# Routing the last chunk of tokens through the experts' blocks, and single chunks through the shared expert, in a GRU and mixture-of-experts kernel

## The reference, cut to what matters

```python
# x: (8, 256, 512), cond_2048: (8, 512); a GRU over 256 steps, then a mixture of experts on its 2048 states
def cell(h, x):
    gi = x @ W_ih + b_ih
    gh = h @ W_hh + b_hh
    r = sigmoid(i_r + h_r); z = sigmoid(i_z + h_z); n = tanh(i_n + r * h_n)
    return (1.0 - z) * n + z * h
...
topk_w, topk_ids = top_k(softmax(x @ w_gate), 2)          # 8 experts, 2 for each token
topk_w = topk_w / sum(topk_w)
gu = einsum('th,ehf->etf', x, w_gate_up)                  # 512 -> 2 * 256 for each expert
eo = einsum('eti,eih->eth', silu(g) * u, w_down)
routed = einsum('te,eth->th', combine, eo)
shared = silu_and_mul(x @ w_sh_gate_up) @ w_sh_down       # 512 -> 2 * 1024 -> 512
...
y = x + routed + shared
```

## Time and profile before

| | us |
|---|---|
| median of three runs | 1266.33 |
| the runs | 1262.6 to 1267.35 |
| the profiled execution, its device time | 1269.48 |
| its span, first to last instruction | 1267.6 |
| TensorE busy in the span | 1074.9 (85%) |
| VectorE busy | 854.7 (67%) |
| ScalarE busy | 569.2 (45%) |
| GpSimd busy | 226.6 (18%) |
| mean granted TensorE clock | 0.981 |
| share of the 16 DMA engines, GpSimd's queue and SyncE's | 31.9% and 13.4% |

### The profile page before, as it was taken

How to read it: one execution, slowest core, us unless ns; L and a number is a source line. 1 busy time by engine, 2 the same in 40 slices (tenths; PEclk the granted TensorE clock), 3 DMA queues, 4 the chain that set the end, 5 groups by cost and what they waited for, 6 DMA issues and landing times.

```text
span 1267.6 us, 35210 instructions
## 1 busy us (share of the span) xinstructions
PE 1074.9 (85%) x13360; PEld 650.7 (51%) x13360; DVE 854.7 (67%) x3767; ACT 569.2 (45%) x1849; POOL 226.6 (18%) x237
## 2 busy tenths in 40 slices
PE   3789887677988889899899888998899798788997
PEld 2556554455554555455455544554455454444775
DVE  5888887688788787677777775777577667411222
ACT  5755445555454444344444433443344244433332
POOL 0100000201010212211321130113013212342331
PEclk9999999999999999999999998999899999989999
DMA  8923554628164741722371343134314503788652
GB/s 302 411 68 110 209 196 151 138 102 301 38 239 157 192 124 24 261 72 51 39 261 27 60 134 144 19 62 168 107 18 77 217 20 87 270 245 248 185 130 43
DMA packets 66442, 180.74 MB, mean 143 GB/s; under 512 B 7579, under 2 KB 40129, under 8 KB 58817
## 3 DMA queue, kind: packets, MB, share of 16 engines
q0 software_dynamic: 24960, 119.25, 31.9%
q1 hardware_dynamic: 41312, 59.24, 13.4%
HBM read 135.18 MB, written 52.08 MB: 148 GB/s over the span
## 4 chain that ended last, share of the span: by engine, by line
PE 44%; DVE 27%; DMA 11%; issue 9%; ACT 6%; POOL 2%; another core or an unknown queue 0%; DVEq 0%; POOLq 0%; SPq 0%; ACTq 0%
PE psG L693 13%; PE psG L699 11%; DMA arena<-hidden_rows,arena 6%; PE psU L756 5%; DVE arena L1047 4%; DVE arena L1045 4%; DVE arena L1051 3%; PE psU L766 3%; ACT arena L1455 3%; DVE arena L1054 2%; PE psS L825 2%; DVE arena L1056 2%; DVE arena L1064 2%; DVE arena L1068 2%; PE psD L778 2%
## 5 line engine op out<-in xcount | busy, mean ns | idle before, releaser
L693 PE MATMUL psG<-arena 128*32 128x384 f16 x4096 | 216.5, 332 | 95.7 <-DVE arena L1068 89.1
L1451 ACT ACTIVATE arena<-arena 128x32 f32<-128x32 f32 x256 | 58.5, 228 | 343.5 <-DVE arena L1049 339.4
L699 PE MATMUL psG<-arena 128*32 128x384 f16 x4096 | 211.8, 327 | 0.0
L756 PE MATMUL psU<-arena 128*128 128x256 f16 x1536 | 203.1, 279 | 0.2 <-DVE arena L941 0.2
L1045 DVE STREAM_TRANSPOSE arena<-psG 128x128 f32<-128x128 f32 x256 | 80.9, 316 | 176.7 <-PE psG L699 167.8
L693 PEld LDWEIGHTS psG<-arena 128*32 128x32 f16 x4096 | 86.7, 97 | 200.1 <-DVE arena L1068 163.8
L756 PEld LDWEIGHTS psU<-arena 128*128 128x128 f16 x1536 | 148.7, 100 | 51.1 <-issue 12.5
L1661 POOL DMA_INDIRECT y<-arena x53 | 84.6, 1597 | 373.0 <-ACT arena L1565 235.8
L699 PEld LDWEIGHTS psG<-arena 128*32 128x32 f16 x4096 | 110.3, 98 | 57.9 <-issue 1.6
L1047 DVE STREAM_TRANSPOSE arena<-psG 128x256 f32<-128x256 f32 x256 | 104.0, 406 | 0.0
L778 PE MATMUL psD<-arena 128*128 128x512 f16 x384 | 96.4, 382 | 0.0
(11 more groups left out here) (178 smaller groups left out, 1631.3 us busy)
## 6 DMA issues: line engine op xcount, KB each, us to landing
arena<-wgu POOLq DMA_DIRECT2D x32, 512.0 KB, 6.8
expert_weights<-arena POOLq DMA_DIRECT2D x9, 1536.0 KB, 5.7
arena<-expert_weights SPq DMA_DIRECT2D x8, 1536.0 KB, 8.3
gi_scratch<-arena SPq DMA_DIRECT2D x84, 128.0 KB, 2.0
arena<-gi_scratch SPq DMA_DIRECT2D x14, 768.0 KB, 6.6
arena<-wd POOLq DMA_DIRECT2D x16, 512.0 KB, 5.3
arena<-x SPq DMA_DIRECT2D x8, 512.0 KB, 3.8
hidden_rows<-arena SPq DMA_DIRECT2D x15, 256.0 KB, 3.1
```

Source lines behind the costliest of these rows:

```text
L693: e.matmul(psG[32 * j:32 * j + 32, 0:384], prev[:, c, 2:6].rearrange("p q n -> p (q n)"), whv[c][1][:, :, :, 32 * j:32 * j + 32], start=(c ...
L699: r = e.matmul(psG[32 * j:32 * j + 32, 0:384], prev[:, c, 0:4].rearrange("p q n -> p (q n)"), whv[c][0][:, :, :, 32 * j:32 * j + 32], star ...
L756: r = e.matmul(psU[u % 2][:, 256 * gu:256 * gu + N], half(W_GS + ex * 4 + c, pw)[:, o:o + 128], hh[:, 1 - ph, c, 0:N], start=(c == 0 and j ...
```

## The change

- `BOUND` becomes 6, 8, 10, 12, 13, 14, 15, 16, 16. All 16 chunks are routed and filed, chunks 12 to 15 as groups of one. The first seven bounds give the blocks that are sure to be full, 23 (`KS`). Then eight blocks (`STATIC`, to `KD` = 31), one for each expert in fixed order, its next one, full or not; their weights come through `x_weights`. Then eight gathered blocks for what is left (`LAST`, to `NB` = 39), with weights by index.
- All 39 blocks run as blocks did; `HX`, `hx`, `comb`, `x_acc`, `acc_init`, `x_rows` and `y_store` go.
- The shared expert takes chunks 12, 13, 14 and 15 one by one, in units of 128 columns (`SINGLE` = 12): 48 units as before and 32 narrow ones. A narrow unit has one `s_down`.
- Due times: routing of the chunks from 12 on is due some 38 steps early, which puts it first; blocks from the fifth bound on are due 4 steps apart. `LANDS` is 7.0 (was 6.0) for hidden gathers and 4.9 (was 6.0) for adds.
- `weights` of a block that isn't its bound's first must come after its own `hidden`, for the first seven bounds.

```diff
-BOUND = (6, 8, 10, 12, 14, 15, 15)
-LAST_BLOCK = [-((8 * 127 - 256 * q) // 128) for q in BOUND[:5]] + [2 * (NCH - 1), 2 * (NCH - 1) + E]
+BOUND = (6, 8, 10, 12, 13, 14, 15, 16, 16)
+STATIC, LAST = 7, 8
+LAST_BLOCK = [-((8 * 127 - 256 * q) // 128) for q in BOUND[:STATIC]]
+LAST_BLOCK += [LAST_BLOCK[-1] + E, LAST_BLOCK[-1] + E + 8]
 FIRST_BLOCK = [0] + LAST_BLOCK[:-1]
-ND, NB = LAST_BLOCK[-2:]
-NU = 8 * NBLK
+KS, KD, NB = LAST_BLOCK[STATIC - 1:]
+
+SINGLE = 12
+NU = 8 * SINGLE // 2
+US = NU + 8 * (NCH - SINGLE)
...
-GROUPS = [(2 * g, 2 * g + 1) for g in range(NBLK - 1)] + [(NCH - 2,), (NCH - 1,)]
-FILED = NBLK
+def dynamic(k):
+
...
+def downs_by(u):
+
+    return 2 * (u + 1) if u < NU else 2 * NU + u - NU + 1
...
+GROUPS = [(q, q + 1) for q in range(0, SINGLE, 2)] + [(q,) for q in range(SINGLE, NCH)]
...
-             "rows": 5.0, "hidden": 6.0, "weights": 9.0, "add": 6.0, "s_add": 6.0}
+             "rows": 5.0, "hidden": 7.0, "weights": 9.0, "add": 4.9, "s_add": 4.9}
...
+        due = s - 2 if q < SINGLE else s - 39
+        p.add("PE", ("tokens", q), 0.6, [("tokens", q - 1)] if q else [], step=s, due=due, takes=True)
...
+        due = s - 3 if n == 2 else s - 40
...
-        v, n = (u - NU) // 2, (u % 8 if u < NU else u % 2)
-        b = u // 8 if u < NU else NBLK - 1
-        s = 32 * (b + 1)
-        due = s + 3.5 * n if u < NU else s + 28 + 3.5 * (u - NU)
+        p.add("PE", ("logits", g), 0.5 * n, last + [("scales", 0)], step=s, due=due, takes=True)
...
+    for u in range(US):
+        n = u % 8
+        q = 2 * (u // 8) if u < NU else SINGLE + (u - NU) // 8
+        s = 32 * (u // 8 + 1) if u < NU else SUB * (q + 1)
+        due = s + 3.5 * n if u < NU else s + 2.0 * n
...
-            p.add("PE", ("s_unit", u, i), 0.37, before, step=s, due=due)
...
+            p.add("PE", ("s_unit", u, i), 0.37 if u < NU else 0.24, before, step=s, due=due)
...
     for v in range(E):
-        free = [[("down", 26 + v - 2, 1)] if v < 6 else [("s_down", NU + 2 * (v - 6) + 1, 1)], [("ew_store", 7)]][v < 2]
-        p.add("SP", ("x_weights", v), 0, free, step=T, due=T + 2 * v)
...
+        free = [("ew_store", 7)] if v < 2 else [("down", KS - 6 + v if v < 6 else KS + v - 6, 1)]
+        p.add("SP", ("x_weights", v), 0, free, step=T if v < 2 else T - 8, due=T - 8 + 2 * v)
...
-        due = s + 4 + (7.0 if i < 5 else 2.0) * (k - FIRST_BLOCK[i])
-        if i == 6:
-            due = T + 28 + 7.0 * (k - ND)
+            before = [("rank", group_of(i))] if i != STATIC else []
+            before += [("list", i - 1, 0 if i == LAST else 4)] if i else [("scales", 1)]
+            costs = (0.75,) if i == STATIC else (1.2, 1.25, 1.0, 0.5, 0.75) if i < STATIC else (1.45, 1.25, 1.0, 0.5)
+            first = s - 2 if BOUND[i] <= SINGLE else s - 38
+            for part, cost in enumerate(costs):
+                p.add("DVE", ("list", i, part), cost, before if part == 0 else [("list", i, part - 1)], due=first + 0.1 * part)
+            p.add("POOL", ("rows", i), 1.0, [("list", i, 0 if i == STATIC else 2), ("file", group_of(i))] + ([("rows_turn", i - 1)] if i else []), due=first + 1)
+            p.add("PE", ("rows_turn", i), 0.4, [("rows", i)], due=first + 1, takes=True)
+            p.add("DVE", ("rows_out", i), 0.45, [("rows_turn", i), ("scales", 1)], due=first + 1, frees=True)
+        due = s + 4 + (7.0 if i < 4 else 4.0) * (k - FIRST_BLOCK[i])
+        if i == LAST:
+            due += 4 * E
...
+        p.add("ACT", ("turn_out", k), 1.04, [("turn", k)] + ago(2, "up", 3), due=due, frees=True)
+        if not KS <= k < KD:
+            before = [("list", i, 3), ("ew_store", 7), ("gates", 95, 3)]
+            if dynamic(k) >= 4:
+                before += [("down", k - 4 if k < KS or k >= KD + 4 else k - 6, 1)]
+            if i < STATIC and k > FIRST_BLOCK[i]:
+                before += [("hidden", k)]
+            p.add("POOL", ("weights", k), 1.0, before, due=due - 3)
...
+            before = [("turn_out", k), ("x_weights", k - KS) if KS <= k < KD else ("weights", k)] if c == 0 else [("up", k, c - 1)]
...
-        xwt = [W_HH * CH, (W_HH + 6) * CH, wst[2], wst[3], wst[0], wst[1]]
...
+        xwt = [W_HH * CH, (W_HH + 6) * CH, wst[3], wst[0], wst[1], wst[2]]
...
+        def ew_half(k, i, part):
+            at = xwt[(k - KS) % 6] if KS <= k < KD else wst[dynamic(k) % 4]
+            return view(at + CH * i + 1024 * part, 512, F16)
...
-                    e.wait_ge(e_dn, ND - 5 + v)
+                    e.wait_ge(e_dn, KS - 5 + v)
                 elif v > 5:
-                    e.wait_ge(s_dn, 2 * (NU + 2 * (v - 6) + 2))
+                    e.wait_ge(e_dn, KS + v - 5)
                 load(view(xwt[v % 6], 12 * 512, F16), ew_d[P * v:P * (v + 1), :], ld_xw[v % 6])
...
+                n, q = u % 8, 2 * (u // 8) if u < NU else SINGLE + (u - NU) // 8
+                first, width = (0, N) if u < NU else (P * (q % 2), P)
+                gu, c, hh = i // KC, i % KC, hb[q // 2 % NHB]
+                o, ex = (n % 4) * 128, 2 * (n // 4) + gu
+                if i == 0:
+                    e.wait_ge(kept, TB * (u // 8 + 1) if u < NU else SUB * (q + 1))
+                for j, (ph, pw) in enumerate(PROD):
+                    r = e.matmul(psU[u % 2][:, 256 * gu:256 * gu + width], half(W_GS + ex * 4 + c, pw)[:, o:o + 128],
+                                 hh[:, 1 - ph, c, first:first + width], start=(c == 0 and j == 0), stop=(c == KC - 1 and j == 2))
...
+                ps = psD[q % 2]
+                if n == 0:
+                    need(e, s_ev, q - 1)
+                for j, (pa, pw) in enumerate(PROD):
+                    r = e.matmul(ps[:, 0:512], AH[u % 3][:, pa, tc * 128:tc * 128 + 128], half(W_DS + n, pw),
+                                 start=(n == 0 and j == 0), stop=(n == 7 and j == 2))
...
-                    e.wait_ge(ld_w[k % 4], 16 * (k // 4 + 1))
+                    if KS <= k < KD:
+                        e.wait_ge(ld_xw[(k - KS) % 6], 16 * ((k - KS) // 6 + 1))
+                    else:
+                        e.wait_ge(ld_w[dynamic(k) % 4], 16 * (dynamic(k) // 4 + 1))
...
-                if i == 6:
-                    rlink(e.tensor_tensor(t_[0:K], FI[0:K], idf[0:K, 0:K], ALU.mult))
+                if i == STATIC:
+                    rlink(e.tensor_tensor(t_[0:K], PP[0:K], idf[0:K, 0:K], ALU.mult))
...
+                    rlink(e.tensor_scalar(fl8, cnt, 63.5 if i == LAST else -63.5, 1.0 / P, ALU.add, ALU.mult))
...
+                    if i == LAST:
+                        rlink(e.scalar_tensor_tensor(out=av, in0=FI, scalar=-1.0, in1=PP, op0=ALU.add, op1=ALU.subtract))
+                        rlinked()
+                        rlink(e.tensor_scalar(av, av, 0.0, None, ALU.max))
+                    else:
+                        rlink(e.tensor_tensor(av, FI, PP, ALU.subtract))
...
-            def x_acc(v):
-                e.wait_ge(s_dn, 2 * (NU + 2 * v + 2))
-                if v == 0:
-                    e.wait_ge(acc_ready, 1)
-                    e.wait_ge(combined, 1)
-                else:
-                    e.wait_ge(x_sum_, v)
-                e.scalar_tensor_tensor(out=so[1], in0=psD[v % 2][:, 0:512], scalar=cw[:, v:v + 1], in1=so[1],
-                                       op0=ALU.mult, op1=ALU.add).then_inc(x_sum_, 1)
...
-            def hx(m):
-                e.wait_ge(kept, T)
-                e.wait_ge(g_w, T)
-                hh = hb[(NBLK - 1) % NHB]
-                e.activation(HX[m][:, 0:KC, P:2 * P], hh[:, 1, :, P:2 * P], ACT.Copy).then_inc(hx_hi, 1)
-                e.activation(HX[m][:, KC:2 * KC, P:2 * P], hh[:, 0, :, P:2 * P], ACT.Copy).then_inc(hx_lo, 1)
...
-                e.wait_ge(picked, boundary_of(k) + 1)
+                e.wait_ge(picked, boundary_of(k) + (1 if k < KS else 0))
...
+                need(e, e_dn, k - 5 if KD <= k < KD + 4 else k - 3)
+                d = dynamic(k)
+                e.indirect_dma_start(view(wst[d % 4], 12 * 512, F16), None, ew_d[:, :],
+                                     by(widx[:, d:d + 1])).then_inc(ld_w[d % 4], 16)
...
```

More of the change, by code:

```diff
@@ new lines, in make_plan @@
+        listed = [("list", i, 0) for i in range(STATIC) if group_of(i) == g - 1]
+        p.add("PE", ("counts", g), 0.15 + 0.15 * n, [("choose", g)], due=due, takes=True)
+        p.add("DVE", ("rank", g), 0.95 + 0.2 * n, [("counts", g), ("choose", g)] + listed, due=due, frees=True)
+        p.add("DVE", ("record", g), 1.0, [("rank", g), ("route_w", g)] + ([("file", g - 2)] if g > 1 else []), due=due)
+        p.add("POOL", ("file", g), 1.3 * 2 * n, [("record", g), ("rows_init", 0)], due=due)
@@ L238, in make_plan @@
[L238 to L246 removed]
+                before += [("sw_low", 11), ("scales", 0)] if q == 0 else []
```

292 lines of the change are left out of this document (79 added, 213 removed).

## The result

The changed kernel takes 1255.0 us (median of six runs, 1250.0 to 1259.3); the kernel before, beside it, 1266.0. The ratio is 0.992 with an interval of 0.989 to 0.995: faster by 0.8%, where 1226 us (3.2% faster) was predicted with a range of 1206 to 1254. The profiled execution spans 1251.8 us, before 1267.6.

What follows compares the result with a forecast made beforehand. It took the recurrence as set by a VectorE chain plus four gather waits, and the second tail as TensorE bound. 1269.5 - 24.6 + 1 - 16.9 = 1229.0, 3.2 above the median: 1226 us, range 1206 to 1254.

Steps and rivals of the forecast that it cites:

- Part 1: Recurrence: weights queued behind hidden gathers remove all four TensorE waits, -24.6 us, with 1 us added for VectorE.
- Rival C: Recurrence: the waits stay, since a first block's weights still go ahead of its rows; 1250 us, chance 0.09.
- Part 2: TensorE's work: fewer expert passes and more routed blocks give -27.5 us; narrow shared matmuls at 0.055 us change nothing.
- rival B: Shared expert: narrow matmuls take 81 ns each, +12 us in the tail to +20 for all; 1242 us, chance 0.07.
- Part 3: Last recurrence steps: 87 of 126 offered cost units fit in steps 208 to 255, leaving the tail 129 us of work.
- rival E: Recurrence steps: the planner fills more of them, tail 13 us shorter; 1213 us, counted within the forecast's 0.68.
- Part 4: Tail: other work covers chunk 15's routing, gaps take 20 us, whole tail 158.8 us against 175.7, -16.9.
- Rival D: Tail: gathers load the queue, less far than adds setting the pace, 7.5 us per block; 1253 us, chance 0.08.
- Rival A: Tail: serial adds into y set the pace, 9.1 us per block, kernel slower; median 1279 us, chance 0.08.
- The signs named beforehand: Whole kernel: no long late steps or row waits, narrow matmuls 0.055 us, adds 6 us apart, TensorE over 0.85 busy in tail.

Runs made afterwards that it cites:

- e9: Kernel before plus the order rule alone (weights of all but a bound's first block after its hidden gather, first five bounds): 1242.7 us, 0.981 of before.
- e6: Changed kernel with the sixteen shared units of chunks 14 and 15 due spread over the whole tail: 1236.0 us, 0.977 of before.
- e4: Changed kernel without the weight gathers of the last eight blocks, which compute with weights already there: 1285.6 us in a slower session, 0.991 of before.
- e13: Changed kernel without the adds of the eight static blocks: 1291.5 us in a slower session, 0.997 of before.
- e1: Kernel before plus the order rule alone, the same kernel as e9, in a slower session: 1289.9 us, 0.994 of before.
- e2: Changed kernel without the order rule, in a slower session: 1305.4 us, 1.006 of before.
- e10: Changed kernel without the order rule, the same kernel as e2, in a faster session: 1273.3 us, 1.005 of before.
- e12: Changed kernel, chunk 15's shared units due 2 steps apart from tail step 16, last blocks' rows gathered and turned 8 steps earlier: 1234.7 us, 0.975.
- e14: e12 without the adds of the eight static blocks: 1281.6 us in a slower session, 0.988 of before.

## Why the prediction missed

**Part 1, order of gathers: right.** The waits of the recurrence on hidden rows went, but for one of 0.3 us; its last step ends at 1064.9, predicted near 1068. e9 measures the rule by itself at 24.0 us, predicted 24.6. The estimate of 2.2 us on top of each wait was made from one step and holds for the four: in the trace of before they take 9.34, 10.97, 9.91 and 10.07 us, together 24.7 over four of 3.89. Rival C (the waits stay) falls.

**Part 2, TensorE's work: right.** Busy 1047.0 us against 1074.9 (27.9 less, predicted 27.5). The agreement is closer than it can claim to be, since busy time grows with time at the lower clock: the same work has 1040.9 us in e6, and that of before 1061.8 in e9. The 24 narrow matmuls above start within 1.34 us, 0.056 each, so rival B falls, and with it the 81 ns of the Trainium skill (TensorE: Matmul & The Clock Gate, section Back-to-back issue gap) for this kernel's pairs of 128 columns: the trace disagrees over runs of 24.

**Part 3, what the steps hold: a little better than predicted.** The changed planner's own order places 99 of its cost units in steps 208 to 255 where I took 87, so the tail starts with blocks 21 and up: 119 us of work, not 129. That was rival E, and alone it would have made the time 10 us shorter. The routing took a little more than estimated (20 to 26 us up to the hidden rows): the row list came 22.6 us after the last step and the first static gather was issued 25.1 after it, at 1090.02, so with 3.3 us of landing some 28. Other work covered that. But the row list's transpose stood in TensorE's order ahead of shared units that were ready, so it cost 4.9 us in spite of the cover, and the lower clock behind it 2.4.

**Part 4, the tail: the step that failed.** "I take 1 us per block, 20 us" came out at 59: with 10 us less work and 1 less of closing that is the tail's 28 us. The first stretch alone used up 17 of the 20. I had the number from the first tail of before, where ten blocks had 10 us of gaps beside their two late gathers. There shared units stood between the blocks, and after it the eight static experts filled TensorE. The change takes that cover away: the shared units are due at the tail's start and run out at 1144.7, and thirteen blocks follow bare, 7.6 us apart (down steps from 1150.39 to 1241.58) and not 5.8. I counted work that covers the routing, and did not ask what covers the blocks themselves once that work is used up. In the prediction's terms: a bare block has 7.6 - 4.55 = 3.05 us of gaps and not 1. e6 shows that the place of the units matters: the same work in another order, -19.4 us, with the gathers moved by it too.

**Late rows** are the second half of the miss. Part 1's insight, that weights ahead of rows make the transpose wait, was not carried to the last group, which the rule leaves out: three waits, 11.4 us together, and by e4 18 us with their clock. Rival D named the loaded queue and 7.5 us per block, 1253 us; the pace was 7.6 and the time 1255. Its number was right partly by luck: the loaded queue is half of what a bare block lost (1.6 of 3.05 us), and the other half, the uncovered copies, no rival had. It also took sixteen blocks at that pace where there are thirteen, behind a first stretch that it priced without gaps and that has 17 us of them. Rival A falls: adds did not set the pace (e13 gives 9 us back through the gathers, not through their own chain).

**The signs named beforehand.** Those of parts 1 to 3 came: no step behind the first hundred is longer than 5 us, and 18 units, 2.25 chunks' worth, were open at the last step. Those of part 4 didn't. TensorE was to be over 0.85 busy up to the last down step: it was (68.28 + 67.63) / 178.2 = 0.76. The adds were to be at most 6 us apart in the last 90 us: they are 5.5 to 12.6, 7.2 on the mean. "Idle over 5 us at once behind the first static block": yes, once, 5.20 us. The DMA share, named at 0.9 for the adds as the pace, was 0.68.

## What to carry to other kernels

Work that fills an engine between dependent steps is worth its place, not only its amount: ask of a tail in which order the filler runs out, and price the steps behind that point with all their waits uncovered (here 7.6 us a block against 4.55 of work). A due time in a planner moves more than its own piece: read the order of every queue again before calling an experiment one of a single cause. When a large transfer is moved behind a small one because the small one is waited for, apply it to every place where both share a queue, and count adds and gathers on one queue together. Measure the parts of a change apart: here one dependence made 24 us and the rest of the change lost about half of it. The best orders found with all work in place, 1234.7 to 1236.5 us (0.975 to 0.977 of before, not told apart by these runs), keep both parts and move the filler, with or without the turns.

## What the chip showed that I had not expected

The slower and the faster sessions differ by 31 us on the kernel before, and by 47 once it has the order rule (e1 and e9, both on a chip with number 8, so the number doesn't tell them apart). It lies in the recurrence (last step at 1111 to 1115 us against 1064 to 1068 with the rule), while the tails agree within 1 us (174.0 and 173.8; 189.9 and 188.9). Between e1 and e9, 31 of the 255 steps are over 0.5 us longer, and they make 41 of the 50 us. In the slower one TensorE pauses inside a step for nothing that the profile shows, here in e1:

```profile
507.26 0.35 PE L700 MATMUL psG<-arena 128*32 128x384 f16 x2 [0.35 <-issue]
508.67 0.37 PE L700 MATMUL psG<-arena 128*32 128x384 f16 x3 [1.06 <-issue]
510.09 0.84 PE L700 MATMUL psG<-arena 128*32 128x384 f16 x7 [1.06 <-issue]
```

Behind the first hundred steps the longer ones take 4.4 to 7.4 us (3.9 to 4.2 in e9), the longest of them at steps 111, 140 and 170; step 46 takes 10.95 (5.03 in e9). The longest in the slower run without the rule, e2, are 7.67 and 8.27 us at steps 119 and 178, where e10 has 10.24 and 9.54: the waits for rows cost less there, and other steps more. That two thirds of the order rule's gain were missing in e1 fits with it. What makes the pauses, and why two sessions have them, was not tried and stays open.

A late gather costs more than its wait: the matmuls behind it run at the lower clock level (in e14, behind a wait of 4.89 us for weights, six of 512 columns have 2.72 us where others have 1.46; in the changed kernel the granted clock is 0.74 in the 20 us from 1164.9). 11.4 us of such waits were worth 18.

Adds into the output, each behind the landing of the one before, follow each other 5.3 to 5.4 us apart with nothing beside them (e12), and one behind two gathers of 1.5 MB landed 10.7 us after its issue (e14), another 12.1 (changed kernel, 1160.06).
